# Low-rank tables split on all partitions, their casts on GpSimd, and a last product in two halves: an exact-precision AdaLN and FFN kernel on one core

## The reference, cut to what matters

```python
q_emb = relu(cond @ W3 + b3)                       # 64 x 512
v = (64 * x + sum(x, axis=1)) * q_emb[:, None, :]  # x is 64 x 64 x 512
x1 = relu(v @ W2 + b2)
w_up = ((w_up_q - 7.5) * repeat(w_up_scale, 64, axis=1)).T      # 512 x 2048
x2 = relu(x1 @ w_up + b_up + x1 @ w_up_lora_a @ w_up_lora_b)
w_down = ((w_down_q - 7.5) * repeat(w_down_scale, 64, axis=1)).T
out = x + x2 @ w_down + b_down + x2 @ w_down_lora_a @ w_down_lora_b
```

## Time and profile before

| | before |
|---|---|
| median of 3 runs | 743.38 us (742.37 to 743.57) |
| the profiled execution's own time | 743.79 us |
| its span in the trace | 742.0 us |
| PE busy | 735.6 us, 99% |
| DVE busy | 556.0 us, 75% |
| ACT busy | 419.9 us, 57% |
| POOL busy | 86.1 us, 12% |

### The profile page before, as it was taken

How to read it: one execution, slowest core, us unless ns; L and a number is a source line. 1 busy time by engine, 2 the same in 40 slices (tenths; PEclk the granted TensorE clock), 3 DMA queues, 4 the chain that set the end, 5 groups by cost and what they waited for, 6 DMA issues and landing times.

```text
span 742.0 us, 9556 instructions
## 1 busy us (share of the span) xinstructions
PE 735.6 (99%) x3258; PEld 608.5 (82%) x3258; DVE 556.0 (75%) x727; ACT 419.9 (57%) x727; POOL 86.1 (12%) x69
## 2 busy tenths in 40 slices
PE   8999999999999999999999999999999999999998
PEld 6888888888888888888888888888888888888886
DVE  6997888788757588676867696868775877757596
ACT  6972484766552565758556275767647263535540
POOL 0065455434310000000000000000000000000000
PEclk9999999999999999999999999999999999999999
DMA  9969989875445986666418896666516796665663
GB/s 287 316 199 357 339 275 306 270 251 194 194 170 166 390 309 227 212 199 198 143 32 268 289 377 226 218 195 197 185 58 200 239 386 216 189 188 189 195 197 129
DMA packets 68946, 170.20 MB, mean 229 GB/s; under 512 B 7650, under 2 KB 8034, under 8 KB 66338
## 3 DMA queue, kind: packets, MB, share of 16 engines
q1 hardware_dynamic: 68034, 168.20, 67.5%
q10 hardware_dynamic: 864, 1.39, 0.6%
HBM read 129.71 MB, written 40.89 MB: 230 GB/s over the span
## 4 chain that ended last, share of the span: by engine, by line
PE 98%; DMA 1%; ACT 0%; DVE 0%; SPq 0%; issue 0%; DVEq 0%
PE ps L1192 32%; PE ps L1193 32%; PE ps L1194 32%; PE ps L1251 1%; PE ps L1206 1%; DMA xt<-in_x 1%; PE ps L1267 1%; ACT xt L409 0%; DVE sums L776 0%; DVE xt_lo L806 0%; ACT xm_hi L421 0%; DVE res L1187 0%; SPq L339 0%; SPq L284 0%; DVEq L90 0%
## 5 line engine op out<-in xcount | busy, mean ns | idle before, releaser
L1192 PE MATMUL ps<-x_hi,ring 128*128 128x512 f32 x672 | 261.4, 389 | 0.0
L1193 PE MATMUL ps<-x_lo,ring 128*128 128x512 f32 x672 | 261.4, 389 | 0.0
L1194 PE MATMUL ps<-x_hi,ring 128*128 128x512 f32 x672 | 261.4, 389 | 0.0
L1194 PEld LDWEIGHTS ps<-x_hi,ring 128*128 128x128 f32 x672 | 126.1, 188 | 26.3
L1192 PEld LDWEIGHTS ps<-x_hi,ring 128*128 128x128 f32 x672 | 126.1, 188 | 26.1
L1193 PEld LDWEIGHTS ps<-x_lo,ring 128*128 128x128 f32 x672 | 126.1, 188 | 26.1
L409 ACT ACTIVATE xt<-xt,gated,gate_n 128x64 f32<-128x64 f32 x216 | 74.7, 431 | 32.7 <-DVE gated L785 32.7
L521 ACT ACTIVATE f<-ps,small_in 128x512 f32<-128x512 f32 x96 | 64.8, 689 | 41.7 <-PE ps L1194 41.7
L977 DVE TENSOR_TENSOR x_lo<-x_sum,x_hi 128x512 fp32r<-128x512 f32 (+1 forms) x96 | 76.6, 818 | 4.2 <-ACT x_hi L559 3.4
L898 DVE TENSOR_TENSOR ps<-s,ps 128x512 f32<-128x512 f32 x48 | 33.2, 692 | 49.7 <-PE ps L1194 49.3
L935 DVE TENSOR_TENSOR res<-ps,res 128x512 f32<-128x512 f32 x71 | 47.4, 686 | 19.7 <-PE ps L1194 19.3
(11 more groups left out here) (94 smaller groups left out, 1035.1 us busy)
## 6 DMA issues: line engine op xcount, KB each, us to landing
ring<-made_w SPq DMA_DIRECT2D x336, 256.0 KB, 3.9
made_w<-made SPq DMA_DIRECT2D x16, 1280.0 KB, 5.6
xt<-in_x SPq DMA_DIRECT2D x32, 256.0 KB, 7.5
code<-in_codes SPq DMA_DIRECT2D x16, 512.0 KB, 8.1
scale<-made_s SPq DMA_DIRECT2D x16, 512.0 KB, 7.7
made_w<-plain SPq DMA_DIRECT2D x16, 512.0 KB, 8.1
res<-in_x SPq DMA_DIRECT2D x4, 2048.0 KB, 10.3
out<-res SPq DMA_DIRECT2D x12, 512.0 KB, 5.6
```

The costliest lines, as they stand in the source:

```text
L1192: pe.matmul(dest, w_hi, a_hi, start=start, stop=False, skip_group_check=True)
L1193: pe.matmul(dest, w_hi, a_lo, start=False, stop=False, skip_group_check=True)
L1194: return pe.matmul(dest, w_lo, a_hi, start=False, stop=stop, skip_group_check=True)
```

## The change

Four things change.

1. A new input `runs` holds the same tables once more, 32 rows cut into four runs of columns and laid on 128 partitions (128 x 768). SP loads it, POOL rounds it (`runs_hi`), DVE subtracts on all 128 partitions (`runs_low`, two instructions of 384 columns), and SP copies the low parts by twelve small DMAs from SBUF to SBUF into their quadrants (`spread`). `lora_low` and both `wide_low` go.
2. The three table roundings move from ACT to POOL.
3. In DVE's list, `x_gate(0, 1)` goes ahead of `x_low(0, 0)`.
4. M7 of the last unit is made as two halves of 256 columns in banks BA and BB of the other set, and no longer on top of M1. DVE adds M1's bank in an addition of its own, then BQ, then each half.

```diff
+            def spread(part):
+                sp.wait_ge(runs_split, 1 if part < 2 else 2)
+                sp.wait_ge(tab_cast, part + 1)
+                width = RUNS[part].stop - RUNS[part].start
+                for c in range(4):
+                    if part == 0:
+                        dest = lora_flat[2 * QUAD:3 * QUAD, c * width:(c + 1) * width]
+                    else:
+                        at = (0 if part == 1 else T) + c * width
+                        dest = wide_flat[QUAD:2 * QUAD, at:at + width]
+                    sp.dma_start(dest.bitcast(F32), runs_lo[c * QUAD:(c + 1) * QUAD, RUNS[part]].bitcast(F32)).then_inc(runs_spread, 16)
...
             copy_scales(slice(0, 2), first_scales_copied)
+            sp.dma_start(raw_runs[:], runs[:]).then_inc(runs_loaded, 16)
             sp.dma_start(raw_tables[0:THREE, 0:2 * D + T], tables[:, 0:2 * D + T]).then_inc(tables_loaded, 16)
...
             load_scale(1)
+            spread(0)
+            spread(1)
             copy_scales(slice(2, UNITS), scales_copied)
             sp.dma_start(raw_tables[0:THREE, 2 * D + T:], tables[:, 2 * D + T:]).then_inc(rest_loaded, 16)
             load_codes(2)
             sp.wait_ge(scales_copied, 16)
             load_scale(2)
+            spread(2)
...
-            act.copy(lora_flat, raw_lora).then_inc(tab_cast, 1)
...
-            act.copy(wide_flat[:, 0:T], raw_wide[:, 0:T]).then_inc(tab_cast, 1)
...
-            act.copy(wide_flat[:, T:], raw_wide[:, T:]).then_inc(tab_cast, 1)
...
+            pool.wait_ge(runs_loaded, 16)
+            pool.tensor_copy(runs_hi[:], raw_runs[:]).then_inc(runs_cast, 1)
+            pool.wait_ge(tables_loaded, 16)
+            pool.wait_ge(warmed, 2)
+            pool.tensor_copy(lora_flat, raw_lora).then_inc(tab_cast, 1)
+            pool.tensor_copy(wide_flat[:, 0:T], raw_wide[:, 0:T]).then_inc(tab_cast, 1)
+            pool.wait_ge(rest_loaded, 16)
+            pool.tensor_copy(wide_flat[:, T:], raw_wide[:, T:]).then_inc(tab_cast, 1)
...
                     pool.wait_ge(x1p_split, KD)
+                    pool.wait_ge(runs_spread, 3 * 4 * 16)
...
+            def runs_low(part):
+                dve.wait_ge(runs_cast, 1)
+                dve.tensor_tensor(runs_lo[:, part], raw_runs[:, part], runs_hi[:, part].bitcast(F32), ALU.subtract).then_inc(runs_split, 1)
...
             w2_low(0)
+            x_gate(0, 1)
             x_low(0, 0)
-            x_gate(0, 1)
...
             x_low(0, 3)
+            runs_low(slice(0, RUNS[1].stop))
             x_sum(0, 5)
...
-            lora_low()
...
-            wide_low(slice(0, T), 2)
...
+            runs_low(RUNS[2])
             add_lora(1)
...
-                if u == 0:
-                    wide_low(slice(T, NH * P), 3)
...
+            to = res[:, 1, 0, :]
+            dve.tensor_tensor(to, ps[4 * (before[1] % 2) + BP][:], to, ALU.add).then_inc(res_summed, 1)
             add_res(*before, BQ)
-
-            to, from_bank = res[:, 1, 0, :], ps[4 * (before[1] % 2) + BP]
-            dve.wait_ge(prod[M7], chain_no(SBS - 1, LAST[-1]) + 1)
-            for half in (slice(0, T // 2), slice(T // 2, T)):
-                dve.tensor_tensor(to[:, half], from_bank[:, half], to[:, half], ALU.add).then_inc(res_done, 1)
+            dve.wait_ge(res_summed, 4 * (SBS - 2) + 6)
+            for bank in (BA, BB):
+                half = slice(T // 2 * bank, T // 2 * bank + T // 2)
+                dve.wait_ge(prod[M7], chain_no(SBS - 1, LAST[-1]) + 1 + bank)
+                dve.tensor_tensor(to[:, half], ps[4 - 4 * (before[1] % 2) + bank][:, 0:T // 2], to[:, half], ALU.add).then_inc(res_done, 1)
...
-            product(SBS - 1, n, M7, BP, False)
...
+            for bank in (BA, BB):
+                wait_bank(pe, bank, SBS - 1, n + 1)
+                half = slice(T // 2 * bank, T // 2 * bank + T // 2)
+                for q in range(2):
+                    z, w = x2_set(SBS - 1, 2 * unit[1] + q), ring[v][:, M7, :, q * P:(q + 1) * P]
+                    mm = three_passes(ps[4 - 4 * v + bank][:, 0:T // 2], w[:, 0], w[:, 1], x2_hi[z][:, X_PLACE[M7], half],
+                                      x2_lo[z][:, X_PLACE[M7], half], q == 0, q == 1)
+                mm.then_inc(prod[M7], 1)
```

More of the change, by code:

```diff
@@ L30, with adaln_ffn @@
 BA, BB, BP, BQ = range(4)
-def adaln_ffn(nc, x, small, w2, codes, scales, tables, out):
+def adaln_ffn(nc, x, small, w2, codes, scales, tables, runs, out):
     SBS, _, KD, _ = x.shape
@@ L156, in adaln_ffn @@
         wide_flat, raw_wide = wide[0:THREE].rearrange("p h c -> p (h c)"), raw_tables[0:THREE, 2 * D:2 * D + NH * P]
+        raw_runs = sb("raw_runs", [P, runs.shape[1]], F32, "res", 4 * (2 * D + NH * P))
+        runs_hi = sb("runs_hi", [P, runs.shape[1]], F32R, "x1", 32768)
+        runs_lo = sb("runs_lo", [P, runs.shape[1]], F32R, "x1", 32768 + 4 * runs.shape[1])
+        RUNS = [slice(0, D // 2), slice(D // 2, D // 2 + T // 4), slice(D // 2 + T // 4, runs.shape[1])]
         raw_w2 = sb("raw_w2", [P, KD, D], F32, "x2")
@@ L187, in adaln_ffn @@
         gate_ready, gate_done, bias_done = sem("gate_ready"), sem("gate_done"), sem("bias_done")
-        w2_cast, w2_split, tab_cast, tab_split = sem("w2_cast"), sem("w2_split"), sem("tab_cast"), sem("tab_split")
+        w2_cast, w2_split, tab_cast, runs_cast, runs_split, runs_spread = (
+            sem("w2_cast"), sem("w2_split"), sem("tab_cast"), sem("runs_cast"), sem("runs_split"), sem("runs_spread"))
+        runs_loaded = sem("runs_loaded")
         x_summed, x_gated, x_shifted = sem("x_summed"), sem("x_gated"), sem("x_shifted")
@@ L366, in _ @@
                 if u == 1:
-                    sp.wait_ge(tab_split, 3)
+                    sp.wait_ge(runs_split, 2)
+                    sp.wait_ge(tab_cast, 3)
                     load_res(0)
@@ L591, in _ @@
             x_high(0, 4)
-            act.wait_ge(tables_loaded, 16)
-            act.wait_ge(warmed, 2)
-            act.copy(lora_flat, raw_lora).then_inc(tab_cast, 1)
             z_tile(0, 0, 0, 0)
@@ L610, in _ @@
                     x1p_high(1, m - 1)
-            act.wait_ge(rest_loaded, 16)
-            act.copy(wide_flat[:, T:], raw_wide[:, T:]).then_inc(tab_cast, 1)
             for u, unit in enumerate(FIRST):
@@ L759, in w2_low @@
                                   ALU.subtract).then_inc(w2_split, 1)
-            def lora_low():
-                rows = slice(2 * QUAD, 3 * QUAD)
-                dve.wait_ge(tab_cast, 1)
-                dve.tensor_tensor(lora_flat[rows, :], raw_lora[rows, :], lora_flat[rows, :].bitcast(F32), ALU.subtract).then_inc(tab_split, 1)
-            def wide_low(part, casts):
-                rows = slice(QUAD, 2 * QUAD)
-                dve.wait_ge(tab_cast, casts)
-                dve.tensor_tensor(wide_flat[rows, part], raw_wide[rows, part], wide_flat[rows, part].bitcast(F32),
-                                  ALU.subtract).then_inc(tab_split, 1)
+            def runs_low(part):
+                dve.wait_ge(runs_cast, 1)
+                dve.tensor_tensor(runs_lo[:, part], raw_runs[:, part], runs_hi[:, part].bitcast(F32), ALU.subtract).then_inc(runs_split, 1)
             def x_sum(s, t):
@@ L1233, in low_rank @@
                 if u == 0:
-                    pe.wait_ge(tab_split, 2)
+                    pe.wait_ge(runs_spread, 2 * 4 * 16)
                     pe.wait_ge(gate_done, KD)
                 elif u == 4:
-                    pe.wait_ge(tab_split, 3)
+                    pe.wait_ge(runs_spread, 3 * 4 * 16)
                 for i in range(2):
@@ L1397, in _ @@
             pe.wait_ge(q_down_done, down_no(SBS - 1, 3, 1) - 8 + 1)
-            product(SBS - 1, n, M7, BP, False)
+            v, unit = n % 2, LAST[-1]
+            pe.wait_ge(w_loaded[v][M7], 16 * ring_round(SBS - 1, n))
+            for bank in (BA, BB):
[6 more added lines that the diff above has]
+                mm.then_inc(prod[M7], 1)
 def kernel(**inputs):
@@ L1436, with in_runs @@
     lora_down = np.roll(a["ffn_w_down_lora_b"], d // 2, axis=1)
+    tables = np.concatenate([by_quadrant(a["ffn_w_up_lora_a"].T, 0), by_quadrant(lora_down, rank), wide], 1)[:3 * QUAD]
+    def in_runs(w):
+        return w.reshape(QUAD, 4, -1).transpose(1, 0, 2).reshape(P, -1)
+    parts = [tables[:QUAD, :2 * d], tables[:QUAD, 2 * d:2 * d + T], tables[:QUAD, 2 * d + T:]]
     arrays = {
@@ L1445 @@
         "scales": scales,
-        "tables": np.concatenate([by_quadrant(a["ffn_w_up_lora_a"].T, 0), by_quadrant(lora_down, rank), wide], 1)[:3 * QUAD],
+        "tables": tables,
+        "runs": np.concatenate([in_runs(w) for w in parts], 1),
     }
```

## The result

The changed kernel takes 746.64 us, the median of 6 runs (746.43 to 749.68), against 742.88 us of 6 runs of the kernel before (742.03 to 743.57). The ratio is 1.0059 with a 95% interval of 1.0048 to 1.0069: 3.8 us slower in the medians, and outside the range forecast. The runs are of two sorts. Four lie at 746.43 to 746.75 with a mean granted clock of 1.00, two at 749.65 and 749.68 with 0.998, which means that the granted clock fell to half for some microseconds in them. The profiled execution is one of the latter, with a span of 747.9 us.

The account below looks back on a forecast made before the run. PE, busy 99% of the span, was taken to bound the kernel. Terms -0.3 + 0.3 + 0.1 + 0.1 = +0.2 us on the median 743.38 gave 743.6 us, range 742.1 to 745.2.

Parts of the forecast that it names:

- The stores behind it: SP's later stores, judged at unit 3: 1.5 us of delay against 1.5 us of slack; +0.1 us, range 0 to +1.1.
- the second entry over 1.5 us: Sign of a wrong forecast: PE's list of waits shows a second entry over 1.5 us.
- the stores come late: Rival: the backlog reaches unit 3 with its full 2.6 us and PE waits 1.1 us, 744.6 us; chance 0.12.
- The tables at the start: Start, up to tile 4: POOL's 2.5 us of casts delay DVE 1.5 us against 1.2 of slack; +0.3 us.
- The spreads: Before `low_rank(0)`: SP issues them at 0.43 to 0.53 us each, landing about 1 us before PE wants them; 0.
- The gate: Start, tile 1: earlier `x_gate` moves ACT's modulation and PE's start 0.3 us earlier; -0.3 us.
- The end: Last unit's M7 in halves: DVE has one more addition and ends last; +0.1 us, from -0.3 to +0.5.

Follow-up runs that it names:

- e14: Kernel before with one added SP wait holding W2's stores until all first products' inputs of the top row are split; 746.52 us.
- e9: e6 with `spread(2)` moved behind W2's stores and the next scale load; 745.05 us.
- e3: Kernel before with SP held back, ahead of the copy of the other units' scales, until the first tables are split; 743.22 us.
- e12: Kernel before with three added casts on POOL, of the changed kernel's sizes, whose results nobody uses; 743.99 us.
- e4: Kernel before with only `x_gate(0, 1)` put ahead of `x_low(0, 0)`; 742.96 us.
- e8: Kernel before with only its three table casts moved to POOL; 745.16 us.
- e15: Changed kernel with W2's stores moved behind the store of unit 9; 745.95 us.
- e10: e9 with the three table casts back on ACT in their old places, POOL keeping `runs_hi`; 746.43 us.
- e6: Changed kernel with `runs_hi` and `runs_lo` in memory POOL's sums do not touch, so DVE, not POOL, waits for the spreads; 749.20 us.
- e2: Changed kernel with the gate's move and the new end undone, leaving the tables' part; 747.93 us.
- e5: Changed kernel with the copy of the other units' scales ahead of the first spreads in SP's queue; 748.72 us.
- e16: Changed kernel with `plain(2)` put behind unit 1's first two full tiles on ACT, and its low part likewise on DVE; 745.85 us.
- e18: e9 with `plain(2)` put behind unit 1's first two full tiles on ACT, and its low part likewise on DVE; 744.61 us.
- e1: Kernel before with only the last product made in halves; 743.50 us.
- e17: Kernel before with `plain(2)` put behind unit 1's first two full tiles on ACT, and its low part likewise on DVE; 743.26 us.

## Why the prediction was wrong

**The stores behind it: the step that failed.** The forecast put +0.1 us here; the wait was 2.3 us, the second entry over 1.5 us that it had named as its sign of being wrong. It saw that W2's stores and the stores of units 0 and 1 would be issued later, and then priced bytes only: of 2.6 us of a full queue it let 1.5 us through, against 1.5 us of slack at unit 3. What mattered was the time of issue, and unit 2. SP's `spread(2)` waits for POOL's last cast, which waits for the rest of the tables, whose load was issued behind the first spreads, and W2's stores stand behind `spread(2)`: 28.64 became 40.96. The queues did not absorb the delay: they stood mostly idle at 25 to 29 us (0.96 became 0.26), and W2's bytes met unit 0's store instead. `e14` shows that W2's late stores alone make the wait (746.52, 1.6 us), and `e9` that it goes from the profile when they are early (32.12). The slack could have been read at unit 2. In the seven kernels of this table with a wait, PE's start there follows ACT's start of `plain(2)` by 4.9 to 5.2 us:

| kernel | store of unit 0 issued | plain(2) starts | PE starts unit 2 | of it wait |
|---|---|---|---|---|
| e3 (up) | 46.03 | 51.20 | 56.68 | 0 |
| before (fallen) | 44.86 | 51.48 | 58.20 | 0 |
| e9 | 47.26 | 52.34 | 58.23 | 0 |
| e12 (fallen) | 47.54 | 52.56 | 58.31 | 0 |
| e4 (late start) | 47.12 | 52.74 | 57.79 | 0 |
| e8 (late start) | 47.64 | 53.88 | 58.98 | 0.9 |
| e14 (fallen) | 45.28 | 54.69 | 59.87 | 1.6 |
| e15 | 47.51 | 54.91 | 59.76 | 1.6 |
| e10 | 45.72 | 55.11 | 60.20 | 1.3 |
| e6 | 47.39 | 55.41 | 60.57 | 2.4 |
| e2 (late start) | 47.85 | 55.72 | 60.88 | 2.4 |
| changed (late start) | 48.72 | 56.35 | 61.51 | 2.3 |

So in the profile before, `plain(2)` could be 58.2 - 5.1 - 51.48 = 1.6 us later for nothing. That slack too is the fall's: in an up execution PE wants unit 2 at 56.68 (`e3`), which leaves 56.68 - 5.1 - 51.20 = 0.4 us. In the changed kernel `plain(2)` was 4.9 us later, and PE itself 1 us. The rival "the stores come late" named the right transfers with 0.12 of chance, but by their bytes, at +1.1 us at most and one unit too far on.

**The tables at the start: right delays, wrong slack.** Casts of 2304 elements took 1.23 + 1.39 + 1.07 = 3.7 us instead of 2.5. DVE lost (1.31 - 0.68) + (1.52 - 0.68) = 1.5 us, which is what the forecast took. The reduction, which has one input, kept its 0.68 us beside a cast (18.98, with the cast of 18.46). The Trainium skill ("SBUF — State Buffer", section "SBUF: two separate sides") states a block for a whole instruction between VectorE with two SBUF inputs and a GpSimd instruction that reads SBUF; these rows agree with it. What was wrong was the 1.2 us of slack behind it. It was read at PE's tile 4 at 23.53, and that PE had been slowed by the fall of the earlier trace rows. In an up execution of a kernel near the one before (`e3`) tile 4 begins at 21.90 and its subtraction ends at 21.46; of these 0.4 us the new subtraction takes 0.5, so no slack is left. `e9`, with the changed start, has tile 4 at 23.06: +1.16 us, where the forecast had -0.3 for the gate and +0.3 for this, together 0. `e12` shows the same by itself, +1.0 us up and +0.2 fallen.

**The spreads.** They landed in time for `low_rank(0)`, as said, and without much to spare: 2 us later in `e10`, PE waited 1.4 us. Four of them took 2.48 and 3.03 us to issue, 0.6 to 0.8 each, not 0.43 to 0.53.

**The gate.** PE's tile 1 begins at 13.10 to 13.28 in the profiles of `e5`, `e6`, `e9`, `e10`, `e15`, `e16` and `e18`, which have it, against 13.58 to 13.83 in those of the kernel before, `e1`, `e3`, `e12`, `e14` and `e17`: about 0.5 us earlier (-0.3 forecast), as ACT's modulation begins at 9.63 (`e5`), 9.70 (`e16`) and 9.81 (`e9`) instead of 10.16. The four profiles with a late start, that of the gate alone (`e4`) among them, have 14.53 to 14.78 and show nothing of it. It is used up before tile 4 wherever the casts are there.

**The end.** +0.1 us forecast, 743.50 against 743.38 measured, which is inside the interval, and DVE is gapless as described. M7's halves came 0.12 us apart, 12 x 0.12 = 1.44.

**The sum now.** For up executions: 742.99 + 1.2 (start) + 2.3 (unit 2) + 0.1 (end) = 746.6, measured 746.43 to 746.75. The three terms are worked out after the fact, from other executions, so this shows that they suffice and is no test. With the clock's fall behind the wait 1.7 us of work are added, 748.3, as in `e6`'s profiled run with the usual start (748.31), which leaves 1.4 of the 749.65 open. The late start of the profiled one is of that size, and 0.9 us of it still stand at unit 2 (61.51 against 60.57 in `e6`); whether the run of 749.65 began late too is not recorded.

**What stays open.** Why unit 0's store took 5.0 us in `e9` and 7.3 us in `e15`, issued at 47.26 and 47.51 behind nearly idle queues. Single runs of `e9` (743.92 to 747.22) and `e15` (744.19 to 746.59) are so wide that the same kernel may have both, and a profile shows one of them; but `e18`, in which this store can no longer hold PE at unit 2 through ACT's order, is nearly as wide (743.86 to 746.24). Why PE starts late in some executions is open as well. No version with the spreads came under the kernel before; `e4_gate` and `e17_before_swap` equal it.

## What to carry to other kernels

When an instruction with a wait goes into an in-order DMA queue, price the time of issue of everything behind it, not its bytes. A later issue can be free (5 us in `e3`) or not (10.5 us of W2's stores in `e14`): whoever uses the full queue next may pay. Follow each late transfer to the buffer that it frees, and from there to whatever stands behind that wait in an engine's list; here, moving that list's order mostly moved the place of payment (0.7 us came back in `e16`, 745.85 against the 746.5 of the changed kernel's up runs). And read slack at the start only in an execution whose clock is at the level that the forecast assumes: here 1.2 us of slack were the shadow of a clock that had fallen.
